# Moving the overflow loop ahead of the late expert blocks, and alternating the output banks of the last projections, in a two-layer gated cross-attention kernel

## The chip, the cores and the metric

The kernel runs on one core of one Trainium2 chip. The metric is device time in microseconds for one execution of the whole kernel; lower is better. Engines are named as the profile names them: PE (matrix multiply), PEld (its weight load), DVE (VectorE), ACT (ScalarE), POOL (GpSimd), SP (the queue of plain DMAs); a name with a q (DVEq, POOLq) is that engine's instruction queue.

## The reference: what is computed

Four residual updates of `x` (4 batches of 256 tokens, 256 columns) follow each other: a graph attention, a dense gated feed-forward layer, a learned sparse attention, and a mixture of 8 experts of which each token uses 2. The change lies in the last:

```python
scores = x @ gate_w.T                                   # 1024 tokens, 8 experts
mult, sel = _masked_sampling_omp(scores)                # 2 experts of each token, and their factors
h = silu(einsum('th,efh->etf', x, w1)) * einsum('th,efh->etf', x, w3)     # 256 -> 512
y = einsum('etf,ehf->eth', h, w2)                       # 512 -> 256
coef = (one_hot(sel, 8) * mult[..., None]).sum(axis=1)
out = x_before + tanh(g_ffn[1]) * einsum('te,eth->th', coef, y)
```

## The kernel before, in words

The kernel computes each expert only for the tokens that chose it. Tokens are sorted on the chip into blocks of up to 128 tokens of one expert. For a block, POOL gathers the tokens' normalised rows from DRAM by an indirect DMA (`gather`, L687), PE turns them (`turn_x`, L2057), multiplies them with the expert's two up weights (`up1` and `up3`, 16 matmul records each, L2071), ACT takes the silu of the first (L976), DVE multiplies the two (`gate`, L1713), PE makes the down product (`down`, 8 records, L2095), ACT scales it by each token's factor (`scale_y`, L1000), and POOL adds the 128 rows to the output in DRAM by an indirect DMA that accumulates (`scatter`, L707).

There are three kinds of blocks:

- Early blocks 0 to 7, one of each expert, with tokens of the first half of the batch.
- Late blocks 8 to 15, one of each expert again (`STATIC = 16`).
- Overflow halves: tokens that fit in neither. A unit holds two halves of 64 tokens, each with an expert that is known only at run time, so each unit's weights are first copied into rooms of its own (`own_weights`, L1729) from an offset that the engine reads into a register (`expert`, L510, a TENSOR_LOAD). Units are worked off in pairs by a hardware loop whose count, at least one, is read at run time (`pairs_in_use`, L485). In this run it goes round once. Each unit has two scatters of 64 rows (`scatter_over`, L730) and fetches the rows of a later unit (`fetch_over`, L715).

Two scatters may name the same token, and each reads its rows, adds and writes them. So every scatter waits until the one before it has landed (`pool.wait_ge(scattered, ...)`): all 8 early, 4 overflow and 8 late scatters form one chain.

The order of each engine's work is written out by hand: the lists `PE_ORDER`, `ACT_ORDER`, `DVE_ORDER` and `POOL_ORDER` up to the middle of block 7, then plain loops. The constant `AT` is the number of blocks that stand ahead of the overflow loop. Before the change `AT = 10`: blocks 0 to 9, the loop, blocks 10 to 15. In the tail loop, block j's slot on PE is `up1(j)`, `turn_x(j + 1)`, `up3(j)`, `down(j - 1)`. All down products but that of block `AT - 1` go to one PSUM bank, each to the half j % 2 of it (`y_bank`), and `down(j)` waits until ACT has read the product before it:

```python
return Y_BANK + 1 if j == AT - 1 else Y_BANK      # y_bank
if 1 <= j != AT - 1:                              # down
    pe.wait_ge(y_scaled, j)
```

Blocks are identified in the trace by counting back from the end: the last three `down` products are at 205.37 (block 14) and 207.92 us (block 15), and the blocks before them stand 5.5 us apart; block 9's is the last ahead of the loop (161.11), block 8's 159.16, block 6's 148.12.

Of the kernel before, what the change touches and what calls it, by code (L numbers as in the profile page):

```python
# [6 lines left out]
ALU = mybir.AluOpType  # L7
# [3 lines left out]
P = 128  # L11
# [22 lines left out]
AT = E + 2  # L34
# [28 lines left out]
def build(nc, x_in, ctx2_in, g_xattn, g_ffn, gamma, w0_in, w0T_in, b0_in, w1_in, w1T_in, a_in, b1_in,  # L63
# [5 lines left out]
    with ctx:  # L69
# [3 lines left out]
        def sem(name):  # L73
# [387 lines left out]
                     ("gate", 5), ("shares", 1), ("gate", 6), ("coefs", 1), ("gate", 7)]  # L461
# [5 lines left out]
                      ("scatter", 0), ("scatter", 1), ("scatter", 2), ("scatter", 3), ("gather", 8), ("scatter", 4), ("gather", 9),  # L467
                      ("scatter", 5), ("gather_over", 0), ("gather_over", 1), ("scatter", 6), ("gather", 10), ("gather", 11), ("scatter", 7),
                      ("gather", 12), ("gather", 13), ("scatter", 8), ("gather_over", 2), ("gather_over", 3), ("scatter", 9),
                      ("gather", 14), ("gather", 15)]  # L470
# [34 lines left out]
        def y_bank(j):  # L505

            return Y_BANK + 1 if j == AT - 1 else Y_BANK

# [78 lines left out]
        def _(pool):  # L587
# [104 lines left out]
            def scatter(j):  # L692
# [5 lines left out]
                if j == E:  # L698
                    pool.wait_ge(out_stored[2], 16)
                    pool.wait_ge(out_stored[3], 16)  # L700
# [19 lines left out]
            def gather_over(u):  # L720

                if u >= 2:
                    pool.wait_ge(over_x_done, u - 1)
                fetch_over(ids[1][:, E + u:E + u + 1], u % 2)
# [26 lines left out]
            pool.wait_ge(list_ready, 4)  # L751
            pairs = pairs_in_use(pool)
# [14 lines left out]
            for j in range(AT, STATIC):  # L767
                scatter(j)
# [6 lines left out]
        def _(act):  # L775
# [244 lines left out]
            act.wait_ge(eoff_ready, 1)  # L1020
            with act.Fori(0, pairs_in_use(act)) as i:
# [23 lines left out]
        def _(dve):  # L1045
# [661 lines left out]
            def gate(j):  # L1707
# [5 lines left out]
                dve.tensor_tensor(hh[me], th[:, me, :], PS[:, 2 + me, :], ALU.mult).then_inc(gated, 1)  # L1713

            def gate_over(u, q):
# [4 lines left out]
            steps = dict(split_bias=split_bias, onehots=onehots, odds=odds, shares=shares, tokens=tokens, ranks=ranks, spare=spare_slots, ids=take_ids,  # L1720
                         coefs=coefs, experts=experts, gate=gate, top=top_rows, hot=hot_rows, lead=lead_check, flag=graph_flag, add_graph=add_graph, spread=spread, guess=guess_rows,
                         move=move, keep=keep, attn_scale=attn_scale, attn_out=attn_out, scales=scales, index=index, scale_down=scale_down,
# [533 lines left out]
```

## Time and profile before

| what | value |
| --- | --- |
| median of 3 runs | 223.6 us (223.42 to 223.99) |
| the profiled execution's own time | 224.26 us |
| its span, first to last instruction | 222.2 us |
| PE busy | 202.9 us (91%) |
| DVE, ACT, POOL busy | 133.6, 85.6, 86.1 us |
| granted PE clock over the span | 0.977 |
| PE busy after 210 us of the span | 0.00 us |

The span leaves 2.06 us of the execution outside. Line numbers L are those of the kernel before. PE's busy time is the sum of pipelined records, so it doesn't say that PE sets the end; what ended last is read from the chain of waits.

### The profile page before, as it was taken

To read this page: it belongs to the slowest core of one execution; us is meant where nothing else is said; L and a number is where in the kernel's file an instruction comes from. 1 tells how busy PE (TensorE), PEld (TensorE's weight loads), DVE (VectorE), ACT (ScalarE), POOL (GpSimd) and SP (SyncE) were. 2 spreads that over 40 slices of the span, in tenths; PEclk is the share of its full clock that TensorE was granted. 3 is DMA by queue.
4 is the path that set the end of the run, shared out by engine and by line. 5 is a ranking of instruction groups with operands and counts; after the bars stand their busy time and mean duration, and the time that the engine had idled before them with its cause. 6 is when DMAs were issued, how large, how long until landed. Compare 5 with 4: busy or idle time off the path is not lost.

```text
span 222.2 us, 3821 instructions
## 1 busy us (share of the span) xinstructions
PE 202.9 (91%) x1282; PEld 158.6 (71%) x1282; DVE 133.6 (60%) x460; ACT 85.6 (39%) x188; POOL 86.1 (39%) x107
## 2 busy tenths in 40 slices
PE   8999979999999989999989999999999999999600
PEld 7787754444885347779979989999953799999400
DVE  3598697999979969997886595925136311111100
ACT  2678652998002364034271272212245332221100
POOL 8065317420011110072822234466768447224320
PEclk9999999999999999999999999999999999999955
DMA  5748317139998135535350231322322010222230
GB/s 175 223 164 242 107 57 242 47 119 418 415 420 330 47 113 204 206 89 192 107 168 1 32 41 21 67 37 41 81 46 48 26 13 8 28 24 25 22 39 7
DMA packets 16796, 26.07 MB, mean 117 GB/s; under 512 B 4095, under 2 KB 12422, under 8 KB 16775
## 3 DMA queue, kind: packets, MB, share of 16 engines
q1 hardware_dynamic: 11328, 20.14, 25.0%
q0 software_dynamic: 4064, 5.25, 13.5%
q10 hardware_dynamic: 1382, 0.41, 0.8%
q8 instruction: 11, 0.18, 0.3%
q14 instruction: 11, 0.08, 0.1%
HBM read 21.34 MB, written 5.51 MB: 121 GB/s over the span
## 4 chain that ended last, share of the span: by engine, by line
PE 34%; DVE 29%; DMA 15%; issue 8%; ACT 7%; POOL 3%; DVEq 1%; POOLq 0%; ACTq 0%
PE PS L2071 12%; DMA out_dram<-a,ids_late 9%; PE PS L2095 6%; DMA out_dram<-zb,sidx 5%; PE PS L1774 3%; PE PS L2106 3%; DVE stat L1066 3%; DVE hT L1458 3%; ACT a L837 2%; PE PS L1838 2%; DVE work L1144 2%; DVE x L1318 1%; DVE mv L1073 1%; PE PS L1825 1%; DVE work L1130 1%
## 5 line engine op out<-in xcount | busy, mean ns | idle before, releaser
L2071 PE MATMUL PS<-hT,e 128*128 128x128 f32 x512 | 62.5, 276 | 1.1 <-ACT hT L966 1.1
L2071 PEld LDWEIGHTS PS<-hT,e 128*128 128x128 f32 x512 | 60.3, 192 | 2.8 <-ACT hT L966 1.9
L1956 PE MATMUL PS<-xnT,e 128*128 128x512 f32 x88 | 39.6, 598 | 1.9 <-DVE hT L1458 0.9
L1713 DVE TENSOR_TENSOR hT<-th,PS 128x512 f32<-128x512 f32 x16 | 11.0, 685 | 38.5 <-PE PS L2071 38.2
L1956 PEld LDWEIGHTS PS<-xnT,e 128*128 128x128 f32 x88 | 16.1, 190 | 22.1 <-issue 17.4
L2095 PE MATMUL PS<-e,hT 128*128 128x256 f32 x128 | 30.6, 382 | 0.8 <-ACT a L1000 0.7
L2095 PEld LDWEIGHTS PS<-e,hT 128*128 128x128 f32 x128 | 23.1, 190 | 3.9 <-issue 1.4
L644 POOL TENSOR_TENSOR rstd<-veps,nhalf 128x2 f32<-128x2 f32 x12 | 8.7, 728 | 39.3 <-DVE veps L1075 39.3
L707 POOL DMA_INDIRECT out_dram<-a,ids_early x8 | 13.4, 1678 | 23.1 <-ACT a L1000 13.2
L1970 PE MATMUL PS<-e,hT 128*128 128x256 f32 x96 | 21.7, 383 | 0.0
L707 POOL DMA_INDIRECT out_dram<-a,ids_late x8 | 12.6, 1573 | 19.3 <-DMA out_dram<-a,ids_late 15.1
L1970 PEld LDWEIGHTS PS<-e,hT 128*128 128x128 f32 x96 | 17.9, 190 | 2.9 <-issue 0.5
L976 ACT ACTIVATE th<-PS 128x512 f32<-128x512 f32 x16 | 9.5, 594 | 19.5 <-PE PS L2071 19.5
L687 POOL DMA_INDIRECT sim<-xn_rows,ids_early x8 | 8.7, 1082 | 19.8 <-DVE ids_early L1682 14.7
L666 POOL DMA_INDIRECT e<-graph_rows,gix x8 | 9.3, 1161 | 9.7 <-DMA graph_rows<-e 8.0
L934 ACT ACTIVATE x<-x,rs 128x256 f32<-128x256 f32 x8 | 4.4, 594 | 21.0 <-DVEq L1490 21.0
L1774 PE MATMUL PS<-ones 128*128 128x128 f32 x64 | 10.8, 326 | 1.0 <-POOL ones L596 1.0
L1000 ACT ACTIVATE a<-PS,coef_late 128x256 f32<-128x256 f32 x8 | 3.8, 474 | 20.2 <-PE PS L2095 17.4
L1000 ACT ACTIVATE a<-PS,coef_early 128x256 f32<-128x256 f32 x8 | 3.8, 473 | 19.3 <-PE PS L2095 16.2
L1774 PEld LDWEIGHTS PS<-ones 128*128 128x128 f32 x64 | 9.5, 230 | 1.8 <-POOL ones L596 1.0
L687 POOL DMA_INDIRECT sim<-xn_rows,ids_late x8 | 8.4, 1048 | 3.7 <-issue 2.1
L1458 DVE SCALAR_TENSOR_TENSOR hT<-th,us,PS 128x512 f32<-128x512 f32 (+1 forms) x12 | 8.9, 745 | 1.3 <-ACT th L927 1.2
(300 smaller groups left out, 320.8 us busy)
## 6 DMA issues: line engine op xcount, KB each, us to landing
e<-e_in SPq DMA_DIRECT2D x24, 512.0 KB, 7.6
x<-x_in SPq DMA_DIRECT2D x2, 512.0 KB, 6.1
graph_rows<-e SPq DMA_DIRECT2D x4, 256.0 KB, 2.1
out_dram<-x SPq DMA_DIRECT2D x4, 256.0 KB, 2.4
xn_rows<-xn SPq DMA_DIRECT2D x4, 256.0 KB, 2.4
e<-gw_in SPq DMA_DIRECT2D x1, 768.0 KB
e<-uw_in SPq DMA_DIRECT2D x1, 640.0 KB
e<-dw_in SPq DMA_DIRECT2D x1, 640.0 KB, 4.5
```

Of the source, the lines that this page charges most:

```text
L644: pool.tensor_tensor(rstd[:, first:first + tiles], veps[:, first:first + tiles], nhalf[:, 0:tiles], ALU.pow).then_inc(rstd_ready, 1)
L666: pool.indirect_dma_start(out=picked[:, t, :], out_offset=None, in_=f_dram[b], in_offset=bass.IndirectOffsetOnAxis(ap=gix[:, t:t + 1], axi ...
L687: pool.indirect_dma_start(out=xg[j % E], out_offset=None, in_=xn3_dram[0:(HN, B * N)[h], :], in_offset=bass.IndirectOffsetOnAxis(ap=ids[h] ...
L707: pool.indirect_dma_start(out=out, out_offset=bass.IndirectOffsetOnAxis(ap=ids[h][:, at:at + 1], axis=0), in_=yv[kept_in(j)], in_offset=No ...
L976: act.activation(th[:, j % 2, :], PS[:, j % 2, :], ACT.Silu).then_inc(silu_ready, 1)
L1458: dve.scalar_tensor_tensor(out=hT[at:P, it, :], in0=th[at:P, n % 2, :], scalar=us[at:P, it:it + 1], in1=PS[at:P, bank, :], op0=ALU.mult, o ...
L1713: dve.tensor_tensor(hh[me], th[:, me, :], PS[:, 2 + me, :], ALU.mult).then_inc(gated, 1)
L1774: pe.matmul(PS[:, bank, 0:P], ones[:, :], ones[:, :], start=True, stop=True)
L1956: mm = pe.matmul(PS[:, bank, :], w[:, k, it * P:(it + 1) * P], xnT[:, h, k, :], start=(k == 0), stop=(k == 1))
L1970: mm = pe.matmul(PS[:, 4 + a // 2, (a % 2) * 256:(a % 2 + 1) * 256], hT[:, it, a * P:(a + 1) * P], dw[:, it, :], start=(it == 0), stop=(it ...
L2071: mm = pe.matmul(PS[:, bank + q, f * P:(f + 1) * P], w[:, k * F + f * P:k * F + (f + 1) * P], xgT[x_at][:, k, :], start=(k == 0), stop=(k ...
L2095: mm = pe.matmul(PS[:, y_bank(j), q * C:(q + 1) * C], hh[q][:, f * P:(f + 1) * P], W2[expert_of(j)][:, f * C:(f + 1) * C], start=(f == 0), ...
```

## The change

1. `AT` becomes 8: the overflow loop stands right behind early block 7, and blocks 8 to 15 all come after it.
2. POOL's order follows: the first two overflow gathers come ahead of the gathers of blocks 8 and 9; gathers 12 to 15 leave the list and are issued one by one in the tail loop, each ahead of a scatter (`gather(j + 4)`, then `scatter(j)`).
3. DVE copies the first unit's weights by two new steps in its list, `("own", 0)` ahead of `("gate", 7)` and `("own", 1)` behind it. Before, the same copies stood around `gate(8)`. Inside the loop, the offsets are read in three places, where before all six were read at its top.
4. In the tail, `down(j - 1)` stands between `turn_x(j + 1)` and `up3(j)`; from block 8 on the down products go to banks `Y_BANK + j % 2`, and `down(j)` waits for `y_scaled` one block further back.
5. Block 15's `up3` is made in two halves of 256 columns in two banks, its gate in two halves of 256 columns, and its down product starts on the first half.

```diff
@@ -31,7 +31,7 @@
 EARLY = (0, 1, 2, 3, 4, 7, 5, 6)
 LATE = (1, 2, 3, 4, 5, 6, 7, 0)
 STATIC = 2 * E
-AT = E + 2
+AT = E
 
 
 HALF = P // 2
@@ -458,16 +458,15 @@
                      ("attn_out", 3), ("moe_stats", 3), ("norm_moe", 2), ("spare", 0), ("norm_moe", 3), ("shares", 0), ("gate", 1),
                      ("choices", 2), ("coefs", 0), ("choices", 3), ("gate", 2),
                      ("onehots", 1), ("gate", 3), ("odds", 1), ("ranks", 1), ("gate", 4), ("tokens", 1), ("ids", 1), ("experts", 0),
-                     ("gate", 5), ("shares", 1), ("gate", 6), ("coefs", 1), ("gate", 7)]
+                     ("gate", 5), ("shares", 1), ("gate", 6), ("coefs", 1), ("own", 0), ("gate", 7), ("own", 1)]
         POOL_ORDER = [("hidden_low", 0), ("hidden_low", 1), ("gather_rows", 0), ("gather_rows", 1), ("norm_var", 0), ("norm_var", 1), ("gather_rows", 2), ("spread", 0), ("spread", 1),
                       ("gather_rows", 3), ("norm_var", 2), ("norm_var", 3),
                       ("attn_stats", 0), ("attn_stats", 1), ("moe_stats", 0), ("moe_stats", 1),
                       ("gather", 0), ("gather", 1), ("gather", 2), ("gather", 3), ("attn_stats", 2), ("attn_stats", 3),
                       ("gather", 4), ("gather", 5), ("gather", 6), ("gather", 7), ("moe_stats", 2), ("moe_stats", 3),
-                      ("scatter", 0), ("scatter", 1), ("scatter", 2), ("scatter", 3), ("gather", 8), ("scatter", 4), ("gather", 9),
-                      ("scatter", 5), ("gather_over", 0), ("gather_over", 1), ("scatter", 6), ("gather", 10), ("gather", 11), ("scatter", 7),
-                      ("gather", 12), ("gather", 13), ("scatter", 8), ("gather_over", 2), ("gather_over", 3), ("scatter", 9),
-                      ("gather", 14), ("gather", 15)]
+                      ("scatter", 0), ("scatter", 1), ("scatter", 2), ("scatter", 3), ("gather_over", 0), ("scatter", 4),
+                      ("gather_over", 1), ("gather", 8), ("scatter", 5), ("gather", 9), ("scatter", 6),
+                      ("gather_over", 2), ("gather_over", 3), ("scatter", 7), ("gather", 10), ("gather", 11)]
 
         order = lambda steps, names: {step: n for n, step in enumerate(s for s in steps if s[0] in names)}
         LN = order(DVE_ORDER, ("norm_var", "attn_stats", "moe_stats"))
@@ -504,7 +503,7 @@
 
         def y_bank(j):
 
-            return Y_BANK + 1 if j == AT - 1 else Y_BANK
+            return Y_BANK + (1 if j == AT - 1 else j % 2 if j >= AT else 0)
 
         def expert(engine, half):
             return engine.value_load(eoff[0:1, half], min_val=0, max_val=(E - 1) * 1024)
@@ -695,9 +694,6 @@
                 if j == 0:
                     pool.wait_ge(out_stored[0], 16)
                     pool.wait_ge(out_stored[1], 16)
-                if j == E:
-                    pool.wait_ge(out_stored[2], 16)
-                    pool.wait_ge(out_stored[3], 16)
                 pool.wait_ge(y_scaled, j + 1)
                 if j >= AT:
                     pool.wait_ge(scattered, pairs * 64 + 16 * j)
@@ -719,6 +715,9 @@
 
             def gather_over(u):
 
+                if u == 0:
+                    pool.wait_ge(list_ready, 2)
+                    wait_rows(1)
                 if u >= 2:
                     pool.wait_ge(over_x_done, u - 1)
                 fetch_over(ids[1][:, E + u:E + u + 1], u % 2)
@@ -749,6 +748,8 @@
                     scatter(*at)
 
             pool.wait_ge(list_ready, 4)
+            pool.wait_ge(out_stored[2], 16)
+            pool.wait_ge(out_stored[3], 16)
             pairs = pairs_in_use(pool)
             with pool.Fori(0, pairs) as i:
                 for q in range(2):
@@ -765,6 +766,8 @@
                     pool.wait_ge(scattered, v * 32 + 16 * (AT + 1))
                     scatter_over(q, 1)
             for j in range(AT, STATIC):
+                if j + 4 < STATIC:
+                    gather(j + 4)
                 scatter(j)
             pool.wait_ge(scattered, pairs * 64 + 16 * STATIC)
             for q in range(2):
@@ -1018,6 +1021,7 @@
                 scale_y(AT - 2 + q)
             copy_x(AT)
             act.wait_ge(eoff_ready, 1)
+            act.wait_ge(coef_ready, 2)
             with act.Fori(0, pairs_in_use(act)) as i:
                 a, b = i * 2, i * 2 + 1
                 experts_b = [expert(act, bass.ds(i * 4 + (2 + n), 1)) for n in range(2)]
@@ -1710,25 +1714,47 @@
                     dve.wait_ge(y_done, j - 1)
                 dve.wait_ge(silu_ready, j + 1)
                 dve.wait_ge(up3_done, j + 1)
-                dve.tensor_tensor(hh[me], th[:, me, :], PS[:, 2 + me, :], ALU.mult).then_inc(gated, 1)
+                if j < STATIC - 1:
+                    dve.tensor_tensor(hh[me], th[:, me, :], PS[:, 2 + me, :], ALU.mult).then_inc(gated, 1)
+                else:
+                    for q in (1, 0):
+                        part = slice((1 - q) * C, (2 - q) * C)
+                        dve.wait_ge(up3_done, j + 2 - q)
+                        dve.tensor_tensor(hh[me][:, part], th[:, me, part], PS[:, 2 + q, part], ALU.mult).then_inc(gated, 1)
 
             def gate_over(u, q):
                 dve.wait_ge(over_silu, u + 1)
                 dve.wait_ge(over_up3_done, u + 1)
                 dve.tensor_tensor(hh[q], th[:, q, :], PS[:, 2 + q, :], ALU.mult).then_inc(over_gated, 1)
+
+            def own_weights(rooms, w, offs):
+
+                for n in range(2):
+                    ins = dve.tensor_copy(rooms[n], w[:, bass.ds(offs[n], 1024)])
+                ins.then_inc(staged_dve, 1)
+
+            first = []
+
+            def own_first(n):
+
+                if n == 0:
+                    for p in range(len(PARTS)):
+                        dve.wait_ge(out_stored[p], 16)
+                        dve.wait_ge(rows_stored[p], 16)
+                    for e in range(E):
+                        dve.wait_ge(experts_loaded[e], 16 * 3)
+                    dve.wait_ge(scores_done, 4)
+                    dve.wait_ge(list_done, 4)
+                    dve.wait_ge(eoff_ready, 1)
+                    first.extend(expert(dve, slice(n, n + 1)) for n in range(2))
+                own_weights((own_w1, own_w3)[n][0], (e1, e3)[n], first)
 
             steps = dict(split_bias=split_bias, onehots=onehots, odds=odds, shares=shares, tokens=tokens, ranks=ranks, spare=spare_slots, ids=take_ids,
                          coefs=coefs, experts=experts, gate=gate, top=top_rows, hot=hot_rows, lead=lead_check, flag=graph_flag, add_graph=add_graph, spread=spread, guess=guess_rows,
                          move=move, keep=keep, attn_scale=attn_scale, attn_out=attn_out, scales=scales, index=index, scale_down=scale_down,
                          hidden_elu=hidden_elu, feat_elu=feat_elu, graph_check=graph_check, norm_var=norm_var,
                          norm_ffn=norm_ffn, ffn_up=ffn_up, ffn_down=ffn_down, attn_stats=attn_stats, attn=attn, moe_stats=moe_stats, norm_moe=norm_moe,
-                         choices=choices)
-            def own_weights(rooms, w, offs):
-
-                for n in range(2):
-                    ins = dve.tensor_copy(rooms[n], w[:, bass.ds(offs[n], 1024)])
-                ins.then_inc(staged_dve, 1)
-
+                         choices=choices, own=own_first)
             for stage in DVE_ORDER:
                 name, *at = stage
                 if name in steps:
@@ -1736,30 +1762,18 @@
                 search(FILL.get(stage, 0))
 
 
-            for p in range(len(PARTS)):
-                dve.wait_ge(out_stored[p], 16)
-                dve.wait_ge(rows_stored[p], 16)
-            for e in range(E):
-                dve.wait_ge(experts_loaded[e], 16 * 3)
-            dve.wait_ge(scores_done, 4)
-            dve.wait_ge(list_done, 4)
-            dve.wait_ge(eoff_ready, 1)
-            first = [expert(dve, slice(n, n + 1)) for n in range(2)]
-            own_weights(own_w1[0], e1, first)
-            gate(E)
-            own_weights(own_w3[0], e3, first)
-            for j in range(E + 1, AT):
-                gate(j)
             with dve.Fori(0, pairs_in_use(dve)) as i:
-                a, b, next_a = [[expert(dve, bass.ds(i * 4 + (u + n), 1)) for n in range(2)] for u in (0, 2, 4)]
+                experts_of = lambda u: [expert(dve, bass.ds(i * 4 + (u + n), 1)) for n in range(2)]
+                b = experts_of(2)
                 dve.wait_ge(over_y_done, i * 2 + 2)
                 own_weights(own_w1[1], e1, b)
-                own_weights(own_w2[0], e2, a)
+                own_weights(own_w2[0], e2, experts_of(0))
                 dve.wait_ge(y_done, AT)
                 gate_over(i * 2, 0)
                 dve.wait_ge(over_up1_done, i * 2 + 2)
                 own_weights(own_w2[1], e2, b)
                 gate_over(i * 2 + 1, 1)
+                next_a = experts_of(4)
                 own_weights(own_w3[0], e3, next_a)
                 own_weights(own_w1[0], e1, next_a)
             for j in range(AT, STATIC):
@@ -2065,8 +2079,8 @@
                 pe.wait_ge(gathered[j % E], 16 * (j // E + 1))
                 turn_rows(xg[j % E], j % 2, xgT_done)
 
-            def up(w, bank, q, x_at, ready):
-                for f in range(F // P):
+            def up(w, bank, q, x_at, ready, parts=range(F // P)):
+                for f in parts:
                     for k in range(2):
                         mm = pe.matmul(PS[:, bank + q, f * P:(f + 1) * P], w[:, k * F + f * P:k * F + (f + 1) * P],
                                        xgT[x_at][:, k, :], start=(k == 0), stop=(k == 1))
@@ -2082,16 +2096,24 @@
                 up(W1[e], 0, j % 2, x_kept_in(j), up1_done)
 
             def up3(j):
-                up(W3[expert_of(j)], 2, j % 2, x_kept_in(j), up3_done)
+                if j < STATIC - 1:
+                    up(W3[expert_of(j)], 2, j % 2, x_kept_in(j), up3_done)
+                else:
+                    for q in (1, 0):
+                        up(W3[expert_of(j)], 2, q, x_kept_in(j), up3_done, range((1 - q) * 2, (1 - q) * 2 + 2))
 
             def down(j):
                 q = j % 2
                 pe.wait_ge(gated, j + 1)
                 if j == 0:
                     pe.wait_ge(x3_ready, 3)
-                if 1 <= j != AT - 1:
+                if j > AT:
+                    pe.wait_ge(y_scaled, j - 1)
+                elif 1 <= j < AT - 1:
                     pe.wait_ge(y_scaled, j)
                 for f in range(F // P):
+                    if j == STATIC - 1 and f == F // P // 2:
+                        pe.wait_ge(gated, j + 2)
                     mm = pe.matmul(PS[:, y_bank(j), q * C:(q + 1) * C], hh[q][:, f * P:(f + 1) * P],
                                    W2[expert_of(j)][:, f * C:(f + 1) * C], start=(f == 0), stop=(f == F // P - 1))
                 mm.then_inc(y_done, 1)
@@ -2185,17 +2207,16 @@
                 down_over(1, (0, 1, 2, 3))
 
             pe.wait_ge(over_x_copied, pairs * 2 + 2)
-            for j in range(AT, STATIC + 1):
-                if j < STATIC:
-                    up1(j)
+            for j in range(AT, STATIC):
+                up1(j)
                 if j + 1 < STATIC:
                     turn_x(j + 1)
-                if j < STATIC:
-                    up3(j)
                 if j == AT + 1:
                     pe.wait_ge(over_y_scaled, pairs * 2)
                 if j > AT:
                     down(j - 1)
+                up3(j)
+            down(STATIC - 1)
 
 
 _OUT = "out_0_dram"
```

What the changed order does, as it stands in the program. First DVE, from the three adds that finish the late factors to the loop (eoff holds the run-time offsets, blocks the number of pairs; x, xnT, wbuf, xn and h0T are rooms for copied weights, e1, e3 and e2 the expert weights; hT<-th,PS is a gate). Before:

```order
L1694 COPY coef_late<-PS 128x24
L1695 TENSOR_TENSOR coef_late<-coef_late,PS 128x24
L1696 TENSOR_TENSOR coef_late<-coef_late,PS 128x24
L1713 TENSOR_TENSOR hT<-th,PS 128x512
L510 TENSOR_LOAD eoff
L510 ISA x2
L510 TENSOR_LOAD eoff
L510 ISA x2
L1729 ISA
L1729 COPY x<-e1 128x1024
```

and after:

```order
L1698 COPY coef_late<-PS 128x24
L1699 TENSOR_TENSOR coef_late<-coef_late,PS 128x24
L1700 TENSOR_TENSOR coef_late<-coef_late,PS 128x24
L509 TENSOR_LOAD eoff
L509 ISA x2
L509 TENSOR_LOAD eoff
L509 ISA x2
L1733 ISA
L1733 COPY x<-e1 128x1024
L1733 ISA
L1733 COPY x<-e1 128x1024
L1718 TENSOR_TENSOR hT<-th,PS 128x512
```

The gate of block 7 moved from ahead of two offset reads and two copies to behind them. Then POOL, from the last overflow scatter (out_dram<-zb) to the late ones (out_dram<-a2), where sim<-xn3_rows is a gather; before:

```order
L730 DMA out_0_dram<-zb,sidx11 1024x256
L753 REGISTER_ALU
L753 COMPARE_AND_BRANCH
L703 ISA
L707 DMA out_0_dram<-a2,ids_late 1024x256
L703 REGISTER_ALU
L707 DMA out_0_dram<-a2,ids_late 1024x256
L703 REGISTER_ALU
```

and after:

```order
L729 DMA out_0_dram<-zb,sidx11 1024x256
L754 REGISTER_ALU
L754 COMPARE_AND_BRANCH
L686 DMA sim<-xn3_rows,ids_late 128x256
L699 ISA
L703 DMA out_0_dram<-a2,ids_late 1024x256
L686 DMA sim<-xn3_rows,ids_late 128x256
L699 REGISTER_ALU
L703 DMA out_0_dram<-a2,ids_late 1024x256
```

Four gathers came in among the late scatters, of which there are now 8 behind the loop instead of 6.

## Rows read from the trace of the kernel before

**Rows 1.** Chain of waits that ended last: start us, us, what.

```profile
174.41 0.48 ACT zb L989
...
175.80 3.12 DMA out_dram<-zb,sidx
...
179.76 2.81 DMA out_dram<-zb,sidx
...
183.40 2.79 DMA out_dram<-zb,sidx
...
186.97 3.10 DMA out_dram<-zb,sidx
...
190.87 3.87 DMA out_dram<-a,ids_late
...
213.81 1.56 POOL out_dram L707
```

**Rows 2.** Timeline of PE: start us, us, engine line op, count.

```profile
148.12 1.89 PE L2095 MATMUL PS<-e,hT 128*128 128x256 f32 x8
...
159.16 1.89 PE L2095 MATMUL PS<-e,hT 128*128 128x256 f32 x8
...
161.11 1.89 PE L2095 MATMUL PS<-e,hT 128*128 128x256 f32 x8
...
163.15 1.94 PE L2106 MATMUL PS<-x,hT 128*64 128x512 f32 x8
...
168.45 0.66 PE L2112 MATMUL PS<-ident,hT 128*128 128x128 f32 x4
...
175.83 2.05 PE L2071 MATMUL PS<-hT,e 128*128 128x128 f32 x16
...
205.37 1.89 PE L2095 MATMUL PS<-e,hT 128*128 128x256 f32 x8
207.92 1.97 PE L2095 MATMUL PS<-e,hT 128*128 128x256 f32 x8 [0.66 <-ACT a L1000]
```

**Rows 3.** Timeline of ACT, block 14's scaled product.

```profile
207.30 0.47 ACT L1000 ACTIVATE a<-PS,coef_late 128x256 f32<-128x256 f32 x1 [2.86 <-PE PS L2095]
```

**Rows 4.** Timeline of DVE around the loop's entry, idle before in brackets.

```profile
146.72 0.18 DVE L1696 TENSOR_TENSOR coef_late<-coef_late,PS 128x24 f32<-128x24 f32 x1
148.42 0.69 DVE L1713 TENSOR_TENSOR hT<-th,PS 128x512 f32<-128x512 f32 x1 [1.53 <-PE PS L2071]
150.67 1.29 DVE L1729 COPY x<-e 128x1024 f32 x2 [1.56 <-issue]
...
159.46 0.69 DVE L1713 TENSOR_TENSOR hT<-th,PS 128x512 f32<-128x512 f32 x1 [3.56 <-PE PS L2071]
164.74 0.69 DVE L1729 COPY wbuf<-e 128x1024 f32 x1 [4.59 <-issue]
...
165.96 1.44 DVE L1729 COPY h0T<-e 128x1024 f32 x2
...
171.09 0.69 DVE L1718 TENSOR_TENSOR hT<-th,PS 128x512 f32<-128x512 f32 x1 [1.13 <-PE PS L2106]
...
172.90 1.29 DVE L1729 COPY x<-e 128x1024 f32 x2
```

**Rows 5.** Line 510, the offset reads on DVE's queue.

```profile
L510 DVEq TENSOR_LOAD <-eoff x8: 300/304/322, 149.3 to 163.9; - x8
```

**Rows 6.** Timeline of POOL, one gather behind another instruction.

```profile
169.19 1.09 POOL L687 DMA_INDIRECT sim<-xn_rows,ids_late  x1 [0.30 <-issue]
```

**Rows 7.** DMA issues: line, count, us from issue to landing.

```profile
sim<-xn_rows,ids_late POOLq DMA_INDIRECT x8, 2.8
```

**Rows 8.** Tile out_dram between 145 and 150 us (one scatter).

```profile
DMA to landing us min/median/max: 3.8/3.8/3.8
```

**Rows 9.** Tile out_dram between 151 and 156 us.

```profile
L707 POOL DMA_INDIRECT out_dram<-a,ids_early x1: 2062/2062/2062, 151.4 to 151.4; - x1
...
DMA to landing us min/median/max: 4.7/4.7/4.7
```

## The prediction

> **What bounds the kernel now.** I read the chain of waits first, backwards from the end. PE is busy for 91% of the span, yet from 175.80 us to the last instruction the chain holds only scatters [rows 1]: 4 overflow ones, started at 175.80, 179.76, 183.40 and 186.97, then 6 late ones from 190.87 to 213.81. Each starts when the one before has landed. Five steps between late scatters take 213.81 - 190.87 = 22.94 us, 4.59 each, of which 3.8 is the landing and the rest the issue behind it. The step from the last overflow scatter to the first late one is 3.90, and from the first overflow scatter to the last late one it is 38.01.
>
> Then the timeline of PE. Its last product, block 15's, ends at 207.92 + 1.97 = 209.89 [rows 2]. Scaled (0.48) and handed to POOL (0.91, from 174.89 to 175.80 [rows 1]), its scatter could have started at 211.3, and started 2.5 us later. So PE isn't what ends the kernel, nor is its stall of 0.66 ahead of that product. What sets the end is when the first overflow scatter starts, and how many scatters stand behind it. Its start goes back to PE: loop entry at 163.15, first unit's product, ACT at 174.41.
>
> **The change, part by part.**
>
> *The loop moves two blocks forward.* Block 8's down product at 159.16 becomes block 6's at 148.12 [rows 2], with the same steps around both. All that hangs on PE comes 11.04 us earlier: loop entry 152.11, first overflow scatter 164.76, if nothing new is late. Two late scatters move behind it and add 2 x 4.59 = 9.18. So the change can win 1.86 us at most, and whatever delays the loop by d takes d back. Break-even is a first overflow scatter at 166.62.
>
> *First delay: DVE at the loop's entry.* Before, DVE sent off gate 7 at 148.42, and its queue then went through nineteen waits and two offset reads, the waits beside that gate, and the copies began at 150.67, 2.25 us behind the gate's start [rows 4]. Now this work hangs behind the last factor add, at 146.72, and gate 7 stands behind the copies: 146.72 + 2.25 = 148.97, two copies 1.29 to 150.26, gate 0.69 to 150.95. PE's product of block 7 may start 0.15 later, at 151.10 (0.15 is the lag from ACT's end, 207.77, to PE's start at 207.92 [rows 2, 3]). Undisturbed it would start at 161.11 - 11.04 = 150.07. Neighbours on DVE overlap by some 0.1 (from 164.74, copies of 0.69, 0.69 and 1.44 would end at 167.56; they end at 167.40 [rows 4]), so I take d = 0.93. Bounds: 0.4, if the waits take only the 1.56 us that DVE stood idle; 1.2, if the queue doesn't start on them before the add has ended. The two copies of `own 1` end near 152.1, before PE needs them.
>
> *Second delay: offsets inside the loop.* Seven reads (one count, six offsets) stood between the gate at 159.46 and the copy at 164.74: 0.75 each, of which a read itself shows 0.30 [rows 4, 5]. Now three stand ahead of the first copies and two ahead of the next pair. From the last copy's start near 151.4: 2.3 to 153.7, copies to 155.0; two reads from 154.3 end at 155.9; the copies to h0T 1.44, to 157.3; the first unit's gate 0.67, to 158.0; PE at 158.15. PE gets there itself at 168.45 - 11.04 + 0.93 = 158.34 [rows 2]. So this delay is 0, but by 0.2 us only; its other end is 1.1, if reads don't run beside copies.
>
> Together d = 0.93: loop entry at 153.04, loop end at 165.72, first overflow scatter at 165.69, last late one at 165.69 + 38.01 + 9.18 = 212.88 against 213.81.
>
> *Gathers 12 to 15 among the scatters.* A gather takes 0.30 + 1.09 of POOL [rows 6] behind a scatter's own 1.56, together 2.95, while the scatter's landing takes 3.8 anyway [rows 1]. Behind the last overflow scatter it is tighter: about 2.9 against 3.10. I put 0.1 on it. What hides the cost is the landing; without that cover it would be 1.39 for each. Gather 12 is the first that could come late: last overflow scatter at 176.86, gather issued near 178.6, landed 2.8 later [rows 7] at 181.4. PE wants it in block 11: 165.72, 3.8 for block 8 (5.52 without a down product), 2 x 5.52, 1.8 of block 11: 182.4. It is in time by 1 us.
>
> *Down product between the ups, two banks, halved last gate.* They shorten PE's end. From 165.72, the 31.3 us of the six tail blocks (175.83 to the end of block 14's product) plus 11.04 give 208.1, and the last gate half with its lags and the product's second half 1.6 (0.15, 0.4, 0.15, 0.9): 209.7. Block 15's scatter could start at 211.1, 1.8 before the chain lets it. So they bring 0 here. Where PE took this lead back they would be worth some 0.66 and half a gate. With down ahead of up3, the gate (0.69) between up3 and the next down is covered by the next up1 (2.05 [rows 2]). The waits for stored rows only moved on POOL.
>
> *A rule against the change.* The scatter at 151.4 ran beside two DVE copies (150.67 to 151.96) and needed 2.06 where the last one needed 1.56, and landed after 4.7 instead of 3.8 [rows 1, 4, 8, 9]. The copies for a next pair, made though none follows, take 2.5 us before (up to 174.19) and now wait for two reads: gate at 171.09 - 11.04 + 0.93 = 160.98, reads to 162.5, copies to 165.0 [rows 4]. They miss the first overflow scatter by 0.7. The Trainium skill, GPSIMD Engine Reference, section 8 (Key points), says that GpSimd shares its SBUF interfaces with VectorE and contends with VectorE instructions in a two-port mode or with two SBUF inputs; the slow scatter of this trace agrees with it. By the rule a meeting costs, and by my times there is none.
>
> **The sum.** -1.86 + 0.93 + 0 + 0.1 + 0 = -0.83, say -0.8. The profiled execution took 224.26 (222.2 and 2.06 around it), so its like becomes 223.4; the median shown is 0.66 lower, so the forecast is 223.6 - 0.8 = 222.8.
>
> **The rivals.**
>
> *DVE is late twice.* Both upper ends hold: d = 1.2 + 1.1 = 2.3 gives +0.5 and 224.1; with d of 1.5 it is 223.3. For it: the second margin is 0.2 us. Against it: the queue did work beside the gate at 148.42: the first read stands at 149.3, 0.2 behind the gate's end, with all nineteen waits done [rows 4, 5]. Mostly no change.
>
> *DVE costs nothing.* d near 0: the full 1.86, 221.8. Against it: the copies stand in the path of gate 7 by program order, and the lower bound is 0.4.
>
> *DVE's spare copies meet the first overflow scatter.* If they run 0.7 later than I have them, its landing grows by up to 0.9: 223.7, no change.
>
> *Gathers are not free: slower.* The scatter that landed after 4.7 us had two gathers behind it. If these and not the copy were the reason, four scatters of the chain take 0.9 more each: -0.8 + 3.6 = +2.8, 226.4. It decides as soon as a gather costs more than 0.4. Against it: the scatter between 145 and 150 us also had two gathers behind it and landed after 3.8 [rows 8, 9], and the overflow scatters with a fetch behind them stepped on by 3.96 and 3.57, those without by 3.64 and 3.90.
>
> *PE's end decides instead.* It would have to lose its 1.8 us, by gather 12 say; then the end moves from there, and 1 us more loss would give 222.8 again plus what exceeds the two margins. The banks and halves would then begin to pay.
>
> **How the numbers follow.** Forecast (d 0.4 to 1.4) 0.55, DVE late twice 0.20, DVE free 0.07, meeting 0.07, gathers 0.07, PE's end 0.04. The forecast's own range is 222.3 to 223.2. A change below 0.3%, 0.67 us, can't be told from none here. Faster: 0.85 of the forecast's cases, all of DVE free, a little of the rest: 0.55. Slower: gathers 0.07 and a tenth of the others: 0.11. The rest, 0.34, is no change. The range for 8 in 10, with the lower bound of the first delay below and late DVE above, is 221.8 to 224.1.
>
> **What would show it.** In the changed profile: the chain's last stretch is 12 scatters, the first overflow one starting at 165.7 (forecast), 164.8 (DVE free) or 166.6 and more (late twice); late steps still 4.59 with gathers between, the last late scatter at 212.9; gate 7 ending near 150.9 behind the copies; PE turning the first unit's gated rows at 158.3; PE done by 209.7 with no stall at its last product. It is wrong if late steps with a gather are longer than 4.8, if the chain's last stretch goes through PE, or if the first overflow scatter starts later than 166.6.

## The result, and the profile after

The changed kernel took a median of 225.28 us (14 runs, 222.57 to 225.95) against 223.59 (14 runs, 222.80 to 223.99): 1.0061 times as long, 95% interval 1.0039 to 1.0083. The ratio leaves out the two longest executions of the changed kernel (225.93 and 225.95), which count as slow since they lie more than 1.5% above its fastest, and compares means; between the medians stand 1.69 us, between those means 1.37. The forecast was 222.8 with a range to 224.1. Its runs also spread three times as wide as those of the kernel before, and that is the first hint: its profiled execution, 222.57, is the fastest of all, and in it every step of the forecast is to be found.

The chain of waits of that execution, from the first unit's scaled product to the last scatter:

```profile
163.80 0.48 ACT zb L992
...
165.20 3.07 DMA out_dram<-zb,sidx
...
169.10 2.87 DMA out_dram<-zb,sidx
...
172.80 2.91 DMA out_dram<-zb,sidx
...
176.50 2.82 DMA out_dram<-zb,sidx
...
180.11 3.71 DMA out_dram<-a,ids_late
...
184.61 3.77 DMA out_dram<-a,ids_late
...
189.17 3.78 DMA out_dram<-a,ids_late
...
212.12 1.54 POOL out_dram L703
```

Each line has the start, the us from there to the landing, and what it is. Against [rows 1]: the same chain of scatters, now 12 of them from 165.20, with landings as before although gathers 12 to 15 run beside four of them. From the first to the last start it takes 46.92 us; 47.19 was forecast.

The timeline of PE of the same execution, which answers to [rows 2]:

```profile
147.50 1.89 PE L2117 MATMUL PS<-e,hT 128*128 128x256 f32 x8
...
150.40 1.99 PE L2117 MATMUL PS<-e,hT 128*128 128x256 f32 x8 [0.79 <-DVE hT L1718]
...
152.55 1.94 PE L2128 MATMUL PS<-x,hT 128*64 128x512 f32 x8
...
157.85 0.66 PE L2134 MATMUL PS<-ident,hT 128*128 128x128 f32 x4
...
165.23 2.05 PE L2085 MATMUL PS<-hT,e 128*128 128x128 f32 x16
...
207.53 1.95 PE L2117 MATMUL PS<-e,hT 128*128 128x256 f32 x8
```

And the timeline of DVE, which answers to [rows 4]:

```profile
146.10 0.18 DVE L1700 TENSOR_TENSOR coef_late<-coef_late,PS 128x24 f32<-128x24 f32 x1
148.46 1.29 DVE L1733 COPY x<-e 128x1024 f32 x2 [2.18 <-issue]
149.67 0.68 DVE L1718 TENSOR_TENSOR hT<-th,PS 128x512 f32<-128x512 f32 x1
...
156.32 0.69 DVE L1728 TENSOR_TENSOR hT<-th,PS 128x512 f32<-128x512 f32 x1 [1.91 <-PE PS L2128]
```

Up to block 6's product this execution runs 0.62 us ahead of the one before (147.50 against 148.12), so 0.62 is to be added to each time below before it is compared. PE waits 0.79 for gate 7, which stands behind the copies. The last product has no stall.

### The profile page after: what moved, and what is told of

Same layout as the page of the kernel before. It is cut to its first block, busy times and chain, and to the rows that moved or that the text cites. A ratio compares the mean times of both kernels' runs of the same rounds, so it can differ in the third digit from the quotient of the medians.

```text
span 220.6 us, 3827 instructions
## 1 busy us (share of the span) xinstructions
PE 201.7 (91%) x1282; PEld 157.9 (72%) x1282; DVE 134.1 (61%) x461; ACT 85.7 (39%) x188; POOL 85.5 (39%) x107
## 4 chain that ended last, share of the span: by engine, by line
DVE 30%; PE 24%; DMA 21%; issue 9%; ACT 7%; POOL 2%; DVEq 2%; SPq 1%; POOLq 0%; ACTq 0%
DMA out_dram<-a,ids_late 12%; PE PS L2085 8%; DMA out_dram<-zb,sidx 5%; PE PS L2117 4%; PE PS L2128 3%; DVE stat L1070 3%; DVE hT L1462 3%; DMA ctx<-ctx_in 2%; ACT a L840 2%; PE PS L1852 2%; DVE work L1148 2%; DVE x L1322 1%; DVE mv L1077 1%; DVE work L1134 1%; DVE top L1144 1%
## 5 line engine op out<-in xcount | busy, mean ns | idle before, releaser
L2085 PE MATMUL PS<-hT,e 128*128 128x128 f32 x512 | 61.7, 276 | 1.1 <-ACT hT L969 1.1
L1718 DVE TENSOR_TENSOR hT<-th,PS 128x512 f32<-128x512 f32 x15 | 10.3, 686 | 36.9 <-PE PS L2085 36.6
L1788 PE MATMUL PS<-ones 128*128 128x128 f32 x64 | 10.3, 316 | 1.0 <-POOL ones L595 1.0
L840 ACT ACTIVATE a<-sim,bar 128x256 f32<-128x256 f32 x16 | 7.9, 496 | 3.8 <-DVE bar L1109 3.8
```

The costliest lines, as they stand in the source:

```text
L840: ins = act.activation(a2[:, t, :], sim[:, t, :], ACT.Sign, bias=bar[:, n, t:t + 1], accum_out=signs[:, t:t + 1])
L1788: pe.matmul(PS[:, bank, 0:P], ones[:, :], ones[:, :], start=True, stop=True)
L2085: mm = pe.matmul(PS[:, bank + q, f * P:(f + 1) * P], w[:, k * F + f * P:k * F + (f + 1) * P], xgT[x_at][:, k, :], start=(k == 0), stop=(k ...
```

## The experiments

The forecast held in the execution that was shown and failed in the median, so I first ran the changed kernel once more, for a second profile, beside three that divide the change. G, D and T are the three theories named in the first expectation; theory C came from these profiles.

**a1, the changed kernel again.** No edit.

> The changed kernel once more, nothing edited. Its profiled execution (222.57 us) agrees with my steps, but its other executions took 224.0 to 225.9, while those of the kernel before lie within 222.8 to 224.0. So something after the loop's entry takes 2 to 3 us more in most executions than in the profiled one. Theory G (gathers): a gather issued behind a scatter makes that scatter land later in most executions; a second profile would show late steps with a gather above 4.8 us. Theory D (DVE copies): DVE's copies meet POOL's scatters at a varying offset, and one or two of them take up to 0.9 more; a second profile shows an overflow scatter of 4 us or more. Theory T (tail): the new order on PE in the tail makes PE late; a second profile shows the last steps released by ACT. Expected time 225.3 under all three.

Measured: 225.50 (8 runs, 223.75 to 226.1), ratio 1.0086 (1.0057 to 1.0116). Its profiled execution took 223.75, with this chain:

```profile
164.86 3.20 DMA out_dram<-zb,sidx
...
168.89 4.43 DMA out_dram<-zb,sidx
...
174.14 2.90 DMA out_dram<-zb,sidx
...
186.11 4.25 DMA out_dram<-a,ids_late
...
191.16 3.77 DMA out_dram<-a,ids_late
...
213.60 1.54 POOL out_dram L703
```

Two landings are long: 4.43 where 2.87 stood, 4.25 where 3.77 stood. POOL issued both as fast as ever (1.47 and 1.57 us), and DVE's last spare copy had ended at 164.59: beside each of the two it had only one gate of 0.69 us, as in the execution after, where the same scatters landed on time. So theory D isn't the cause of either, and theory G doesn't fit the first, an overflow scatter with no gather issued behind it. What the DMA view shows in these places, here from 171.0 to 171.6 us (40 columns: busy share of the 16 DMA engines in tenths, and GB/s by the packets' starts), is this:

```profile
DMA  0900011219000129990012200000000600000100
GB/s 0 137 1 1 1 2 2 3 2 342 0 0 0 1 1 72 137 1093 0 0 1 2 1 0 0 0 0 0 0 0 0 69 0 0 0 0 0 1 0 0
...
q0 software_dynamic: 67, 0.01, 27.0%
q8 instruction: 1, 0.02, 10.5%
```

Queue q0 is the scatter. In the middle of it, at 171.26 (the column with 1093 GB/s), one packet of another queue starts, q8, "instruction": 16 KB, and 10.5% of 16 engines for 0.6 us is 1.0 us of one engine. The page lists 11 such packets in 0.18 MB. The same stands at 188.0 to 188.6, with the packet at 188.27:

```profile
q0 software_dynamic: 23, 0.02, 64.3%
q8 instruction: 1, 0.02, 9.5%
```

Theory C: these are pieces of an engine's program. By it a scatter's rows are spread over the DMA engines, and it has landed only when the last of them has; so one engine held up for 1 us can hold up the scatter, and the chain passes all of it on. The trace doesn't tell which engine a packet ran on.

**a2, gathers ahead.**

```diff
-("gather", 9), ("scatter", 6), ... ("scatter", 7), ("gather", 10), ("gather", 11)]
+("gather", 9), ("gather", 10), ("gather", 11), ("scatter", 6), ... ("scatter", 7), ("gather", 12), ..., ("gather", 15)]
-                if j + 4 < STATIC:
-                    gather(j + 4)
```

> The changed kernel with gathers 10 and 11 moved ahead of scatter 6 and gathers 12 to 15 put behind scatter 7, so that none stands among the late scatters. All else is as changed. Theory G: back to the forecast, 222.7 to 223.2, and narrow. Theories D and T: 225, as wide as the changed kernel.

Measured: 224.39 (223.81 to 225.0), 1.0044 (1.0024 to 1.0065): between the two expectations. With no gather among the late scatters, the overflow scatter at 169.71 landed after 4.05, a q8 piece starting 2.1 us behind it. Theory G falls as the cause of such landings; why the median is 1.1 below a1's this run doesn't show, and by theory C it is that the scatters now start at other moments against the pieces.

**a3, old tail.** The hunks on `y_bank`, the last gate, `up3`, `down` and PE's tail loop undone.

> The changed kernel with the tail of the kernel before: up1, turn, up3, down in each block, one output bank, block 15's up3 and gate in one piece. The loop stays ahead of block 8. Theory T: 222.7 to 223.2. Theories G and D: 225, since PE's end has 1.8 us to spare and the tail decides nothing.

Measured: 224.13 (223.81 to 225.31), 1.004 (1.0018 to 1.0062). Its profiled execution had the longest landing of all, 5.46 us at 185.61, with a piece 3.4 us behind its start:

```profile
185.61 5.46 DMA out_dram<-a,ids_late
```

**a4, new tail only.** The same hunks applied to the kernel before.

> The kernel before with the new tail alone (down product between the ups, two banks, last block in halves); the loop stays ahead of block 10. Theory T: 225 or more. Theories G and D: 223.6, no change, since its chain of scatters has 2.5 us to spare against PE.

Measured: 223.43, ratio 0.9995 (0.9973 to 1.0018). Theory T falls: the tail's edits are worth nothing either way here, as forecast.

**b1 to b6, the code moved.** If the pieces are PE's program, instructions that are never executed must move them. They were put in the branch for the general case, which this run doesn't take (here 32 of them):

```diff
                 with pe.If(r):
                     pe.wait_ge(sim_copied, 4)
                     general_path()
+                    for _ in range(32):
+                        pe.sem_inc(qk_done)
```

> The changed kernel with 32 instructions added to PE's program inside the branch that isn't taken in this run, so none is executed; all that lies behind them moves 2 KB further in PE's code. Theory C (code loading): PE's code arrives in pieces of 16 KB over the same DMA engines (queue q8 on the page); where a piece meets a scatter's rows, the scatter lands 1.2 to 1.6 us late, and the chain takes all of it. In the repeat of the changed kernel pieces came 2.3 us behind the start of an overflow scatter (landing 4.43 instead of 2.9) and of a late one (4.25 instead of 3.8). PE runs through some 88 instructions in 5.52 us, so 32 of them make the pieces come 2.0 us earlier: near 169.2, 186.2 and 202.4, with scatters at 169.0, 184.6 and 198.4 or 202.9, 0.2, 1.6 and 4 us behind their starts. Expected by C: 222.6 to 223.3. Theories G (gathers among the scatters) and T (order of the tail): 225.4, as the changed kernel.

> The same with 16 instructions: pieces 1.0 us earlier, near 170.2, 187.2 and 203.4. The second then comes 2.6 us behind the start of the late scatter at 184.6, the others 1.2 and 0.5 behind theirs. Expected by C: one meeting, 223.5 to 224.5. Theories G and T: 225.4.

> The kernel before with the same 32 instructions in the branch that isn't taken. Its pieces come at 175.4, 188.1 and 204.4, 0.4 ahead of and 1.1 behind starts of overflow scatters and 4.3 behind that of a late one, which cost next to nothing. 2.0 us earlier they come near 173.4, 186.1 and 202.4: the second 2.7 behind the overflow scatter at 183.4, the third 2.3 behind the late one at 200.1. Expected by C: one or two meetings, 224.6 to 226. Theories G and T: 223.4, no change.

> The kernel before with 16 such instructions: pieces near 174.4, 187.1 and 203.4; the third 3.3 us behind the late scatter at 200.1, where the kernel with the old tail showed a landing of 5.46. Expected by C: 224 to 225. Theories G and T: 223.4.

> The changed kernel with 64 instructions in the branch that isn't taken. 32 of them moved the pieces from 171.1, 188.2 and 204.7 to 171.1, 187.1 and 203.6, so half of what I had worked out, and the first not at all. 64 should bring the second and third to 186.1 and 202.6: 1.5 us behind the scatter at 184.6 or ahead of one, and 2.9 behind one. Theory C: the first meeting stays (4.1 to 4.5 on the second overflow scatter), the third piece may bring another: 224 to 225.5. It is of use mainly for more pairs of piece and landing: any landing of 4 us or more must have a q8 piece 1.5 to 3.4 us behind its start.

> The same with 128 instructions, half a piece. The pieces should leave the place near 171 and come near 163, 180, 196 and 212. Theory C: no meeting with an overflow scatter, one at most with a late one: 222.6 to 224. If time and landings don't follow the pieces, Theory C falls.

Measured (starts of pieces and long landings in each one's profiled execution, from the first overflow scatter on):

| kernel | median us | ratio (95%) | q8 pieces, us | landings of 4 us and more: start, landing, piece behind start |
| --- | --- | --- | --- | --- |
| a1, changed | 225.50 | 1.0086 (1.0057, 1.0116) | 171.3, 188.3, 204.9 | 168.89: 4.43, 2.4; 186.11: 4.25, 2.2 |
| b2, + 16 | 224.35 | 1.0018 (1.0001, 1.0034) | 171.1, 187.9, 204.0 | 168.98: 4.54, 2.1 |
| b1, + 32 | 224.10 | 1.0022 (1.0000, 1.0044) | 171.3, 187.3, 203.7 | 169.22: 4.06, 2.1 |
| b5, + 64 | 223.54 | 0.9992 (0.9972, 1.0013) | 168.7, 184.5, 200.9 | 198.76: 4.84, 2.1 |
| b6, + 128 | 223.75 | 1.0011 (0.9985, 1.0036) | 163.9, 179.0, 196.5 | none |
| b4, before + 16 | 224.36 | 1.0020 (0.9997, 1.0043) | 174.4, 185.8, 202.5 | 199.58: 5.15, 2.9 |
| b3, before + 32 | 223.74 | 1.0004 (0.9987, 1.0020) | 173.7, 185.0, 199.9 | none |

Each ratio is against the kernel before, timed beside it. Without one instruction more to execute, the changed kernel loses up to 2 us of its 225.5. The q8 pieces move, those of the other instruction queue, q14, stay (near 162 and 194 to 197 in all changed ones): q8 is PE's program. The second meeting of a1 is gone in b1, b2 and b5, where its piece comes earlier; the first stays in b1 and b2, where its piece didn't move. My arithmetic for how far they move was poor: b1's first piece not at all, its second 1.0 us instead of 2.0, b3's third 4.4. So b1 came out 0.8 above its expectation, b3 0.9 and b5 0.5 below theirs, while b2, b4 and b6 came out within. What the steps between pieces follow besides the address I don't know.

**c1 and c2, a packet of 16 KB put there on purpose.** SP, behind its last waits, in the kernel before (`flat` makes one row of a DRAM tensor; an element count that is prime, 17 or 4099, gave one packet for each copy in the trace):

```diff
+            for j in range(AT, STATIC - 1):
+                sp.wait_ge(scattered, 64 + 16 * (j + 1))
+                for n in (17, 4099):                      # c2: (17, 17)
+                    sp.dma_start(flat(f_dram[0], n), flat(f_dram[1], n)).then_inc(router_loaded, 16)
+                    seen += 16
+                    sp.wait_ge(router_loaded, seen)
```

> The kernel before; behind each of late scatters 10 to 14, once it has landed, SP makes a copy of 68 bytes and then one of 16,396 bytes from DRAM to DRAM, each as one packet, so that the long one should reach its DMA engine some 2 to 3 us behind the start of the next scatter. It stands for a piece of PE's code. Theory C: the scatters that meet it land 0.5 to 1.6 us late; over five of them 3 to 8 us more, 226 to 231. Theories G and T: the chain doesn't care, 223.5.

> The same with both copies of 68 bytes: the same waits, issues and landings on SP, but nothing that holds a DMA engine. Theory C: 223.5, as before. If it is as slow as the one with long copies, the issue of DMAs beside POOL costs the time, and not the length of a packet.

Measured: c1 227.21, 226.64, 227.91 and 223.21 in its four runs, too few and too far apart for a ratio; c2 223.29 (10 runs), ratio 0.9993 (0.9973 to 1.0013). So the long copies don't cost every execution. What they do is read from the profiled ones, 227.21 and 222.94. The chain of c1, late scatters 10 to 14, of which the copies meet the last four:

```profile
190.41 3.87 DMA out_dram<-a,ids_late
...
195.07 4.49 DMA out_dram<-a,ids_late
...
200.35 4.61 DMA out_dram<-a,ids_late
...
205.77 4.55 DMA out_dram<-a,ids_late
...
211.11 4.78 DMA out_dram<-a,ids_late
```

and that of c2, with the same waits and issues and short packets:

```profile
189.69 3.84 DMA out_dram<-a,ids_late
...
194.32 3.71 DMA out_dram<-a,ids_late
...
198.82 3.70 DMA out_dram<-a,ids_late
...
203.33 3.79 DMA out_dram<-a,ids_late
...
207.92 3.78 DMA out_dram<-a,ids_late
```

Up to the first copy the two executions keep the same pace (15.12 and 14.99 us from the first overflow scatter to the first late one). Then four long packets, starting 2.4 to 3.3 us behind a scatter, go with landings of 4.49 to 4.78, 0.7 to 1.0 more than in c2; the fifth, 3.3 behind the last scatter, goes with 3.77, as without it. (The third scatter also has a q8 piece 4.0 behind its start.) That a long packet of another queue can make a scatter late is shown by this pair without PE's code, in one execution of each.

**d1 to d4, the reads early.** To check the forecast's own term for the first delay, eighteen waits and two offset reads were moved behind gate 6, where DVE idles; d2 to d4 add 64, 128 and 192 unexecuted instructions.

```diff
-("gate", 6), ("coefs", 1), ("own", 0), ("gate", 7), ("own", 1)]
+("gate", 6), ("read", 0), ("coefs", 1), ("own", 0), ("gate", 7), ("own", 1)]
+            def read_first(n):            # the waits but list_done, and first.extend(...), from own_first
```

> The changed kernel; the eighteen waits and the two offset reads that stood between the last factor add and the first weight copy now stand behind gate 6, where DVE is idle for 1.7 us. The copies should start near 146.4 instead of 148.5, gate 7 at 148.0 where PE needs it, and PE's product of block 7 no longer waits (0.79 before). All behind it 0.7 to 0.8 us earlier: first overflow scatter 164.4 instead of 165.2. Code pieces move with PE, so the meetings stay as they are. Expected: 225.4 - 0.8 = 224.6. If the delay isn't on the path, 225.4.

> d1 with 64 unexecuted instructions in PE's code. b5 against the changed kernel took 1.8 us off; d1's 0.8 on top: 222.8.

> d1 with 128: b6 (223.75) less 0.8: 222.9. No long landing in the profile.

> d1 with 192, three quarters of a piece: pieces near 158, 175, 191.5 and 208 by b6's steps. Scatters start near 172 and 175.7 (overflow), 188.4 and 207 (late), so 2.9 behind one, 3.1 behind one and 1 behind one: one or two meetings, 223.5 to 225.

Measured: d1 224.63 (1.0041; 1.0022 to 1.0061), d2 222.54 (0.9959; 0.9929 to 0.9989), d3 222.66 (0.9953; 0.9934 to 0.9972), d4 221.79 (0.9927; 0.9898 to 0.9955). DVE in d1:

```profile
146.68 0.18 DVE L1700 TENSOR_TENSOR coef_late<-coef_late,PS 128x24 f32<-128x24 f32 x1
146.79 1.56 DVE L1733 COPY x<-e 128x1024 f32 x2
148.27 0.67 DVE L1718 TENSOR_TENSOR hT<-th,PS 128x512 f32<-128x512 f32 x1
```

The copies follow the add at once, and PE's product of block 7 starts without a wait. d1 to d3 came out within 0.3 us of their expectations, and d1's profiled execution has the two meetings of a1 again, landings of 4.48 and 4.66 with pieces 2.1 and 2.5 behind. d4 was expected at 223.5 or more: pieces came 2.8 and 3.0 us behind two scatters, and neither landed late. d2 to d4 beat both kernels, by 0.4 to 0.7% of the kernel before. Against a1, b5, b6 and e2, which have the same shifts without the early reads, the ratios are lower by 0.0033 to 0.0058, 0.7 to 1.3 us. In d3 one late scatter, block 14's at 206.56, waited for PE's product and started some 0.4 us behind its turn: there PE's end begins to count.

**e1 and e2, the same shift without the early reads.**

> The kernel before with 192 unexecuted instructions in PE's code. If the place of the code alone made d4 fast, this one is fast too, 222.5 or less. By Theory C it is the kernel before with no meeting or one: its own pieces cost it little where they stand, so it can't win more than some tenths: 223 to 224.5.

> The changed kernel with the same shift, without the early reads: d4 plus 0.8, 222.6, which is what the forecast gave the change (222.8).

Measured: e1 223.99 (1.0011; 0.9995 to 1.0026), e2 223.44 (0.9972; 0.9949 to 0.9995). This place of the code makes the kernel before no faster; the gain needs the changed order under it, and most of d4's gain needs the early reads too. e2 lies 0.8 above its expectation.

## Why the prediction was wrong

*What sets the end.* Right: the chain of scatters, in both profiled executions of the changed kernel.

*Two blocks forward, 11.04 us, and 9.18 back.* Right. With the 0.62 added, the loop's entry stands at 153.17 (153.04 forecast) and the first overflow scatter at 165.82 (165.69).

*First delay.* Right in place and size: gate 7 ends at 150.35 + 0.62 = 150.97 (150.95 forecast), PE's product at 151.02 (151.10). The whole delay up to the loop is 1.06 against 0.93. d1, which takes most of it away, is 0.87 faster than a1 in medians, 1.0 by the ratios; their intervals still overlap, and the four pairs together carry it.

*Second delay.* Right that it is 0: the first unit's turned rows start 5.30 us behind the loop's entry, before and after. The margin was larger than I had it, since the reads ran beside the copies: DVE stood idle for 1.91 us ahead of the first unit's gate, at 156.32.

*Gathers, and PE's end.* Right: late steps of 4.50 to 4.64 with a gather between and 4.49 to 4.73 without. PE was done at 209.48 + 0.62 = 210.10 against 209.7, and its last scatter could have started 1.2 us before the chain let it, not 1.8. The rival that made the gathers the danger didn't come true; it had asked the right question, whether a landing stays what it was, about the wrong traffic. DVE's spare copies ended 0.3 us before the first overflow scatter started, where I had 0.7.

*The sum.* It gave -0.8, and the one profiled execution of the changed kernel without a long landing is about that much faster than the profiled one before: 222.57 + 0.62 = 223.19 against 224.26, 1.07. That this one was shown, the fastest of 14, is luck. The step that failed is the one that took the chain from the first overflow scatter to the last late one as a fixed length, 38.01 + 9.18, read from an execution before in which no piece of code met a scatter of that stretch: its pieces come 0.2 us ahead of the start at 175.80, 1.0 behind that at 186.97, 4.3 behind that at 200.08. The change moved the chain against PE's program, so that in a1 pieces come 2.4 and 2.2 us behind starts, and the same length is 48.74 instead of 46.92. Late landings of this kind measured 0.2 to 1.7 us more than usual. The medians ask for a missing term of +2.5 (1.69 measured, -0.83 forecast), but that is what is left over, not a measurement of its own: a1's profiled execution, with two meetings, took 223.75, which is 1.75 below the median of a1. So most executions must lose more than that one did, to larger or more meetings or to something that no profile here caught.

*The rule against the change, and the gathers' rival.* The trace before held a meeting, and I took it for something else. Both passages start from the scatter at 151.4 that landed after 4.7 [rows 9] and blame DVE's copies or two gathers. A q8 piece starts at 153.68, 2.3 us behind it. In b3 and b4, which run the same copies and gathers there but have no piece 2 to 3.5 us behind it, the same scatter landed after 4.2; in the four with one 2.2 to 2.3 us behind (before, a4, c1, c2) after 4.4 to 4.7. So of the 0.9 about 0.4 goes with the copies or gathers and up to 0.5 with the piece; the longer issue, 2.06 us, is there in all of them and is not the piece's doing.

*What stays open.* From the first overflow scatter on, all 12 landings of 4 us or more in 19 profiled executions (all but c1, with its own packets) had a piece 2.1 to 3.4 us behind the start, the mildest of them 4.02 in e2. The bar of 4 us hides smaller ones: e1's first overflow scatter, with a piece 1.7 behind, stepped on after 4.58 instead of 3.96. Earlier in the kernel landings up to 4.2 occur without one at that distance, as in b3. A piece there is not sufficient: 11 scatters had one in that stretch and landed on time, those of the profiled execution after among them (2.4 behind 169.10, 3.4 behind 184.61). Whether the piece lands on an engine that still has rows to move would explain it, and wasn't tried. That the unprofiled executions of the changed kernel are long by such meetings is argued from the shifted kernels and not shown in their own traces. The shifts moved the times together with the pieces, but b6, without a long landing in its profiled execution (222.16), has a median of 223.75 too. Over the places tried, with a1 as the unshifted one, the changed order averages 1.002 and the order before 1.001, so the forecast's gain of 0.8 us came near to being had in the median at one place only (e2, 0.0028 or 0.6 us).

## What to carry to other kernels

When a kernel ends in a chain of DMAs, each waiting for the one before, a long packet of another queue can be on the critical path, an engine's own program among them; the short ones of c2 cost nothing. Look up the instruction pieces in the DMA view beside the chain, and before crediting an edit with some tenths of a per cent, move the code by some unexecuted instructions and time again: here that alone was worth 2 us of 225. Waits and register reads ahead of a step that another engine waits for belong in an idle stretch in front of it; 0.8 us was worked out for that, and four pairs of kernels gave 0.7 to 1.3. A single profiled execution can be the fastest of all, so compare its time with the median before reading the median from it.

## What the runs showed of the hardware that I had not expected

- PE's program arrives in pieces of 16 KB, each one packet of about 1.0 us (10.5% of 16 engines in 0.6 us), one every 15 to 17.5 us in the last blocks (after, a1, b1, b2, b5, b6), and a scatter beside it lands up to 1.7 us late (5.46 instead of 3.8 in a3), or not at all late.
- With a packet of 16,396 bytes put beside it by SP, a scatter landed 0.7 to 1.0 us late in four cases of five (c1); with 68 bytes in none (c2).
- A register read on DVE (0.30 us, 0.7 with what follows it) runs beside DVE's copies: in the execution after, between the last weight copy (150.26 to 151.55) and the next one inside the loop (151.47) no idle time was left for three of them.
